# Experts' lists in another order, and expert 0's tokens in two halves, in a cross-attention and mixture-of-experts kernel

## The reference

```python
xn = xf / rms * norm_weight                      # 4096 x 256
logits = xn @ router_weight.T + router_bias      # 4096 x 16
probs = softmax(logits)
_, idx = jax.lax.top_k(logits.T, 256)            # per expert: 256 tokens
h = gelu(xn[idx] @ fc1_weight.T + fc1_bias)      # 256 x 1024 per expert
y = h @ fc2_weight.T + fc2_bias                  # 256 x 256
output = zeros.at[idx].add(y * gates); output /= sum of a token's gates
x = x + output
```

## Time and profile before

| | |
|---|---|
| median of three runs | 1154.19 us |
| profiled execution | 1155.01 us, its span 1153.2 us |
| PE busy | 1018.4 us, 88% of the span |
| DVE, ACT, POOL busy | 817.6, 669.7, 786.9 us |
| mean granted TensorE clock | 0.948 of full speed |

### The profile page before, as it was taken

One profiled execution on the slowest core, in us unless ns is written; L12 is line 12 of the kernel. 1 busy time (PEld: TensorE's weight loads), 2 busy tenths in 40 slices (PEclk: granted clock), 3 DMA queues, 4 the chain that ended last, 5 costly groups with the idle time before them and its releaser, 6 DMA issues.

```text
span 1153.2 us, 17657 instructions
## 1 busy us (share of the span) xinstructions
PE 1018.4 (88%) x6086; PEld 645.8 (56%) x6086; DVE 817.6 (71%) x1901; ACT 669.7 (58%) x1299; POOL 786.9 (68%) x880
## 2 busy tenths in 40 slices
PE   3779999999999999999998999998750499999996
PEld 2545445545645645554564555444320378999995
DVE  6886867976796786888769757785278756666642
ACT  6566675675586567748656765534424135666662
POOL 3117895896698679679678976977712168777773
PEclk9869999999999999999999999999965599999998
DMA  6020020010002002101200010010127146666652
GB/s 181 1 60 1 1 60 2 1 55 25 20 2 81 22 6 66 30 1 38 62 20 1 3 26 19 1 33 2 38 71 194 46 83 201 207 220 211 221 159 26
DMA packets 73817, 71.95 MB, mean 62 GB/s; under 512 B 38976, under 2 KB 67776, under 8 KB 69632
## 3 DMA queue, kind: packets, MB, share of 16 engines
q1 hardware_dynamic: 66608, 62.05, 17.1%
q0 software_dynamic: 6336, 8.70, 4.2%
q10 hardware_dynamic: 784, 0.07, 0.1%
HBM read 56.98 MB, written 13.83 MB: 61 GB/s over the span
## 4 chain that ended last, share of the span: by engine, by line
PE 73%; DVE 14%; POOL 4%; ACT 4%; issue 2%; DMA 1%; SPq 0%; ACTq 0%; DVEq 0%; POOLq 0%
PE bank L830 38%; PE score_pair L830 17%; PE pair_bank L830 12%; ACT probs L1128 3%; POOL prob_sum L1390 3%; PE bank L863 2%; DVE c_in L1800 2%; PE bank L911 2%; DVE root_t L1489 1%; DVE root_y L1491 1%; DVE maxima L1675 1%; DVE root_t L1490 1%; DVE in_stats L1496 1%; DMA c_in<-in_ctx 1%; DVE qk_nat L1649 1%
## 5 line engine op out<-in xcount | busy, mean ns | idle before, releaser
L1390 POOL TENSOR_TENSOR prob_sum<-prob_sum,probs 128x256 f32<-128x256 f32 x628 | 464.8, 771 | 77.4 <-ACT probs L1128 70.6
L1128 ACT ACTIVATE probs<-score_pair,mask_col 128x512 f32<-128x512 f32 x256 | 161.7, 683 | 117.5 <-PE score_pair L830 101.5
L1682 DVE CUSTOM_DVE_ANT_0 masked_scores<-pair_bank,mask_bias 128x512 bf16<-128x512 f32 x248 | 161.0, 686 | 85.3 <-PE pair_bank L830 84.8
L830 PE MATMUL bank<-probs,v_nat 128*64 128x512 f32 x768 | 206.3, 625 | 0.2 <-ACT probs L1128 0.2
L1675 DVE TENSOR_REDUCE maxima<-pair_bank 128x2 f32<-128x1024 f32 x62 | 75.8, 1223 | 45.9 <-PE pair_bank L830 45.8
L830 PE MATMUL score_pair<-q_hi,k_hi 64*128 64x512 f32 x384 | 91.3, 468 | 19.0 <-ACT probs L1128 17.6
L1128 ACT ACTIVATE probs<-score_pair 128x512 f32<-128x512 f32 x128 | 69.2, 592 | 65.5 <-PE score_pair L830 62.0
L830 PEld LDWEIGHTS score_pair<-q_hi,k_hi 64*128 64x128 f32 x384 | 37.2, 184 | 104.2 <-ACT probs L1128 55.7
L830 PE MATMUL pair_bank<-k_hi,q_hi 64*128 64x512 f32 x372 | 88.6, 471 | 5.4 <-DVE maxima L1675 2.4
L1368 POOL TENSOR_TENSOR z_lo<-z_full,z_hi 128x512 fp32r<-128x512 f32 x32 | 40.8, 1282 | 60.6 <-ACT z_hi L1128 60.6
L1461 POOL DMA_INDIRECT out_x<-y_out,token_index x32 | 55.1, 1722 | 39.1 <-DVE y_out L1985 34.2
(11 more groups left out here) (256 smaller groups left out, 2551.8 us busy)
## 6 DMA issues: line engine op xcount, KB each, us to landing
w_raw<-in_fc SPq DMA_DIRECT2D x16, 1024.0 KB, 4.8
w<-in_fc SPq DMA_DIRECT2D x16, 1024.0 KB
c_in<-in_ctx SPq DMA_DIRECT2D x16, 384.0 KB, 3.4
x_in<-in_x SPq DMA_DIRECT2D x8, 512.0 KB, 5.3
out_x<-x_in SPq DMA_DIRECT2D x8, 512.0 KB, 3.8
rows_scratch<-xr_nat SPq DMA_DIRECT2D x8, 512.0 KB, 3.0
c_in<-in_ctx SPq DMA_DIRECT2D x16, 128.0 KB, 3.4
b_rows<-in_fc_bias SPq DMA_DIRECT2D x16, 128.0 KB, 5.9
```

The source lines that it names most:

```text
L830: return pe.matmul(out, lhsT, rhs, start=start, stop=stop, skip_group_check=True)
L1128: return act.activation(out, a, f, bias=bias, scale=scale)
L1390: last = tt(total[:, half], first[:, half], p[:, half], ALU.add)
L1682: last = dve.tensor_tensor_reduce(masked[:, hh, :], place[:, hh, :], mask_bias[:, 512 * g:512 * (g + 1)], 1.0, MASKED, ALU.add, ALU.max, m ...
```

## The change

Parts 0 and 1 become experts 0 and 1 (64 columns), and the other fourteen (448 columns). Both first lists are made before anything of the others' slots. The chain up to the lists has fewer links: the limit's bits go straight into the tile that PE transposes, the marks read it from PSUM, the count of those above goes into the second rank as one more matmul (`rank(part, 1)`) instead of into two DVE operations. ACT makes one half of the ids for the first two groups (`ids_scaled`), and for group 0 both halves come in two pieces of 16 tiles. `list_join` is one operation, and the sum that it made moves behind the spread.

Expert 0's tokens are turned in halves, and its first four hidden pieces are done once for each half of 128 tokens (`hidden_part`). `order` is cut into `taken`, `order` and `rank`, which stand in other places. `turn_tokens(1)`, `scale_gates`, `renew_rows` and `split(2, 0)` stand ahead of expert 0's second product, `split(2, 1)` behind it. `EARLY` is 2.

```diff
-EARLY = 3
+EARLY = 2
...
-    def first_expert():
-
-        add("order", 1)
-        add("turn_tokens", 0)
-        add("slots", 1)
+    def first_lists():
+
+        add("limits")
+        add("taken", 0, 0)
+        add("order", 0, 0)
+        add("rank", 0, 0)
+        add("taken", 0, 1)
+        add("order", 0, 1)
+        add("rank", 0, 1)
+        add("keep_limits")
+        add("slots", 0)
+        add("list_hot", 0, 0)
+        add("list_hot", 0, 1)
+        add("list_count", 0)
+        add("list_join", 0)
+        add("list_spread", 0)
+        add("gather", 0)
         add("list_hot", 1, 0)
         add("list_hot", 1, 1)
-        for f in range(FT):
+        add("list_count", 1)
+        add("taken", 1, 0)
+        add("list_join", 1)
+
+    def first_expert():
+
+        add("turn_tokens", 0, 0)
+        add("order", 1, 0)
+        add("list_spread", 1)
+        add("gather", 1)
+        for f in range(2):
+            add("hidden_part", 0, f, 0)
+        add("turn_tokens", 0, 1)
+        for f in range(2, 4):
+            add("hidden_part", 0, f, 0)
+        add("rank", 1, 0)
+        for f in range(4):
+            add("hidden_part", 0, f, 1)
+        add("taken", 1, 1)
+        add("order", 1, 1)
+        add("rank", 1, 1)
+        add("slots", 1)
+        for f in range(4, FT):
             add("hidden", 0, f)
-            if f == 4:
-                add("list_count", 1)
-                add("list_join", 1)
-            elif f == 5:
-                add("list_spread", 1)
-                add("gather", 1)
-                add("scale_gates")
-                add("list_hot", 2, 0)
-                add("list_hot", 2, 1)
-                add("gather_gates", 0)
-                add("gather_gates", 1)
+        add("turn_tokens", 1)
+        add("scale_gates")
+        add("renew_rows")
+        add("split", 2, 0)
+        for part in range(2):
+            add("list_hot", 2, part)
+        for e in range(EARLY):
+            add("gather_gates", e)
         for c in range(2):
             for n, f in enumerate(OUT_ORDER[c]):
                 add("expert_out", 0, c, f)
...
                 elif c and n == 6:
                     add("list_spread", 2)
                     add("gather", 2)
-                    add("gather_gates", 2)
-                    add("renew_rows")
             add("gate", 0, c)
-            if c == 0:
-                add("turn_tokens", 1)
+        add("split", 2, 1)
 
     for r in range(SEARCH_ROUNDS):
         add("search", r)
         if r in FIRST_SPLITS:
             add("split", *divmod(FIRST_SPLITS.index(r), 2))
-    add("order", 0)
-    add("slots", 0)
-    for part in range(2):
-        add("list_hot", 0, part)
-    for piece in ("list_count", "list_join", "list_spread"):
-        add(piece, 0)
-    add("gather", 0)
+    first_lists()
...
             if at == (9 if e == 1 else 4):
                 for c in range(2):
                     add("scatter", e - 1, c)
-            if at == 1 and e == 1:
-                add("split", 2, 0)
-            if at == 9 and e + 1 < E:
+            if at == 9 and 2 < e + 1 < E:
                 add("split", e + 1, 1)
             if at == 13 and e + 2 < E:
...
+        def limits():
+            on.wait_ge(attention_done, 4)
+            on.wait_ge(choice_consts, 1)
+            on.wait_ge(*order_ready.at("wide"))
+            pe.transpose(bank[1][:, 0:E], wide[:], ident[0:E, 0:E]).then_inc(searched.sem, 1)
+
+        def rank(part, n):
+
+
             experts = experts_of[part]
             columns = slice(experts.start * NT, experts.stop * NT)
-            if part == 0:
-                on.wait_ge(attention_done, 4)
-                on.wait_ge(choice_consts, 1)
-                on.wait_ge(*order_ready.at("wide"))
-                pe.transpose(bank[1][:, 0:E], wide[:], ident[0:E, 0:E]).then_inc(searched.sem, 1)
-            else:
+            flat = lambda t: t[:].rearrange("p e j -> p (e j)")[:, columns]
+            if part:
                 on.wait_ge(*slots_made.at(0))
-            flat = lambda t: t[:].rearrange("p e j -> p (e j)")[:, columns]
-            for n, taken in enumerate((above, equal)):
-                on.wait_ge(*order_ready.at("tiles", part, n))
-                mm(order_bank[n][:, columns], before[:], flat(taken), True, False)
-                mm(order_bank[n][:, columns], all_ones[:], earlier[:, columns], False, True).then_inc(searched.sem, 1)
-                if n == 0:
-                    totals = running[:].rearrange("p (e j) -> p e j", j=NT)[:, experts, NT - 1]
-                    mm(list_bank[:, total_place][:, experts], all_ones[:], totals, True, True).then_inc(searched.sem, 1)
+            on.wait_ge(*order_ready.at("tiles", part, n))
+            if n:
+                totals = running[0][:, experts, NT - 1:NT].broadcast_to([P, experts.stop - experts.start, NT])
+                mm(order_bank[n][:, columns].rearrange("p (e j) -> p e j", j=NT), all_ones[:], totals, True, False)
+            mm(order_bank[n][:, columns], before[:], flat(kinds[n]), n == 0, False)
+            mm(order_bank[n][:, columns], all_ones[:], flat(earlier[n]), False, True).then_inc(searched.sem, 1)
...
+        def list_hot(g, part):
+
+            if part and g < 2:
+                on.wait_ge(*rests_marked.at(g))
+                for at in list_tiles(g):
+                    func(hot_ids[:, at, 0:1, 0, :], hot_lo[:, at, 0:1, :], ACT.Identity,
+                         scale=token_in_tile[:, 0:1]).then_inc(ids_scaled.sem, 1)
+
...
+        def up(e, f, c=None):
+
             i = e % 2
-            on.wait_ge(*xe_emptied.at(e))
+            on.wait_ge(*xe_emptied.at(*token_key(e, c)))
             for n in range(2):
                 on.wait_ge(*w_lo_made.at(e, n))
-            n = e * FT + f
+            n = hidden_turn[e, f]
             if n >= 4:
                 on.wait_ge(*h_made.at(*hidden_order[n - 4]))
-            to, cols, n = hidden_bank[n % 4][:, 0:CAP], slice(f * P, (f + 1) * P), 0
+            tokens = slice(0, CAP) if c is None else slice(c * P, (c + 1) * P)
+            to, cols, n = hidden_bank[n % 4][:, tokens], slice(f * P, (f + 1) * P), 0
             for half in range(2):
                 for w, x in ((w1_hi, xe_hi), (w1_lo, xe_hi), (w1_hi, xe_lo)):
-                    last = mm(to, w[i][:, half, cols], x[i][:, half, :], n == 0, n == 5)
+                    last = mm(to, w[i][:, half, cols], x[i][:, half, tokens], n == 0, n == 5)
                     n += 1
-            last.then_inc(hidden_filled.sem, 1)
+            return last
+
+        def hidden(e, f):
+            up(e, f).then_inc(hidden_filled.sem, 1)
+
+        def hidden_part(e, f, c):
+            last = up(e, f, c)
+            if c:
+                last.then_inc(hidden_filled.sem, 1)
...
+
+        def limits():
+
+            on.wait_ge(attention_done, 4)
+            on.wait_ge(choice_loaded, 16 * N_CHOICE)
+            ts(wide[:].bitcast(U32), low_bits[0:E, :].broadcast_to([E, P]), high_bits[0:E, :], limit_flip[0:E, :],
+               ALU.bitwise_or, ALU.bitwise_xor).then_inc(order_ready.sem, 1)
+
+        def keep_limits():
+
+            on.wait_ge(*searched.at("limits"))
+            dve.tensor_copy(limit[:], bank[1][:, 0:E]).then_inc(limits_kept, 1)
...
-            parts = list_parts[0:16 * n, 0:n]
             on.wait_ge(*listed.at(g))
-            settle(tt(parts.rearrange("p i a x -> p (i a x)"), list_bank[0:16 * n, 0:32 * n],
-                      own_block[0:16 * n, 0:n, :].rearrange("p i x -> p (i x)"), ALU.mult))
-            stt(list16[0:16 * n, 0:n, :], parts[:, :, 1, :], float(P), parts[:, :, 0, :], ALU.mult,
-                ALU.add).then_inc(joined.sem, 1)
+            tt(list_parts[0:16 * n, 0:n].rearrange("p i a x -> p (i a x)"), list_bank[0:16 * n, 0:32 * n],
+               own_block[0:16 * n, 0:n, :].rearrange("p i x -> p (i x)"), ALU.mult).then_inc(joined.sem, 1)
 
```

More of the change, by code:

```diff
@@ L770, in _build @@
             if at[1]:
-                ids_made.will(at[0])
+                for part in range(len(list_tiles(at[0]))):
+                    ids_made.will(at[0], part)
+                    if at[0] < 2:
+                        ids_scaled.will(at[0], part)
+            else:
+                rests_marked.will(at[0])
         elif kind == "list_count":
@@ L783, in _build @@
             xe_emptied.will(*at)
[L784 to L788, removed]
+        elif kind == "hidden" or kind == "hidden_part" and at[2]:
+            hidden_filled.will(*at[:2])
+            hidden_order.append(tuple(at[:2]))
+            h_made.will(*at[:2])
+            if in_parts(*at[:2]):
                 h_hi_made.will(*at)
@@ L818, in _build @@
     searched.will("limits")
-    for part in range(2):
-        for piece in (("order", part, 0), ("totals", part), ("order", part, 1)):
-            searched.will(*piece)
-    experts_of = (slice(0, 1), slice(1, E))
-    order_bank, total_place = bank[5:7], slice(P, P + E)
+    for kind, *at in expert_plan:
```

(28 more changed lines are left out.)

146 lines of the change are left out of this document (80 added, 66 removed).

## The result

The changed kernel takes 1160.97 us (median of 19 executions, 1156.57 to 1164.46), the one before, beside it, 1155.52 (19, 1153.41 to 1157.71): ratio 1.0047, 95% interval [1.0035, 1.0059]. The prediction, 1152.3 with a range to 1157.4, was wrong: the forecast did not come, and the rival in which the clock comes late came, larger than I had priced it. The profiled execution took 1160.71 us, its span is 1158.9.

The account below looks back on a forecast made before the run. PE, busy throughout from 968.9 us, bounds, so expert 2's start decides: 4.4 us gained, 2.6 left after halves, a 4.4 us stall; expert 2 0.4 earlier, expert 3 1.85 earlier; 1153.15 profiled, 1152.3 us median, range 1148.3 to 1157.4.

Parts of the forecast that it names:

- the rival in which the clock comes late: Expert 0's hidden pieces: half passes do little to raise the clock; 4.2 us more, 1156.5, at upper bounds 1158.3; chance 0.27.
- Index and first pass: Chain to the first list and gather: index 1.0 us earlier; PE needs only the first gather, first pass 4.4 us earlier.
- Price of a half pass: Expert 0's passes of 128 tokens: 0.115 us each at full clock, 0.213 at half clock; 24 passes more.
- The rival that prices halves by columns: PE takes half passes at 0.107 and 0.06 us; time 1149.8, or 1148.5 without the SBUF collision; chance 0.22.
- Less 0.4 because the clock should rise about 5 us after the first pass: Expert 0's hidden pieces: clock rises short of the 24th half pass, 0.4 us off; sum 11.8, end at 923.1.
- The collision with the gates: POOL's subtraction from `split(2, 0)` holds a two-input DVE operation in the gates: 1.3 us more (bounds 0 and 2.4).
- The stall at the count: PE, ready at 929.5, waits for list 2's ids; count begins at 933.95; a stall of 4.4 us.
- I charge 1.8: Clock lost in the stall before expert 1: 1.8 us (bounds 0 and 2.3), first pass of expert 1 at 938.5.
- Expert 1 in 14.1 us, expert 2 not waiting: Expert 1 takes 14.1 us (bounds 13.4 and 15.4); POOL is ready, so expert 2 starts at 952.6.
- the 16 that the prediction named as a sign of being wrong: Expert 1's duration: the prediction called itself wrong if it took under 13 us or over 16.

Follow-up runs that it names:

- half5: all_four with expert 5's 8 hidden pieces in 96 half passes of 128 columns instead of 48 whole ones; 1153.69 us, ratio 0.9986.
- wide_halves: Changed kernel with the same 48 passes in the place of expert 0's half passes, each with 256 columns; 1156.18 us, ratio 1.0001.
- split20_later: Changed kernel with the split of expert 2's first half of weights moved behind the gathers of the gates; 1157.79 us, ratio 1.0015.
- turn1_later: Changed kernel with expert 1's tokens turned behind expert 0's first 16 second products, as in the kernel before; 1155.31 us, ratio 1.0005.
- fill_short: Changed kernel with 9 unused products (18 passes) on PE in its wait for list 2's ids; 1154.98 us, ratio 0.9998.
- whole0: Changed kernel with expert 0's first four hidden pieces in whole passes of 256 tokens, both turns still halves; 1156.02 us, ratio 0.9993.
- all_four: Changed kernel with expert 0 in whole passes, expert 1's tokens turned later, and expert 2's and 3's first-half weight splits moved later; 1148.49 us, ratio 0.9942.
- three_wide: all_four with expert 0 in half passes again, but each 256 columns wide; 1148.78 us, ratio 0.9943.
- three_halves: all_four with expert 0 in half passes again; 1152.59 us, ratio 0.9979.

## Why the prediction was wrong, step by step

- **Index and first pass: right.** The index was 0.9 us earlier (forecast 1.0; 8.3 instead of 9.1 behind the common zero), the first pass 4.3 us earlier (forecast 4.4). That PE needs only the first gather held.
- **Price of a half pass: right.** 0.21 us at half clock, 0.112 at full (I took 0.115). The Trainium skill's figure in TensorE: Matmul & The Clock Gate, Back-to-back issue gap, 81 ns, did not hold for this form; half5 shows 112. The rival that prices halves by columns is refuted.
- **"Less 0.4 because the clock should rise about 5 us after the first pass": this is the step that failed.** It rose 14.2 us after it, behind the last half pass, although PE had no gap in all that time. I had read 4.0 us of whole passes in the kernel before and carried them to half passes; wide_halves shows that the columns made the difference. The hidden pieces ended at 928.0 instead of 923.1 (4.4 us net of the shifted zero); the rival's price was 4.2.
- **The collision with the gates: right in kind,** 1.0 us for 1.3 (split20_later).
- **The stall at the count: right,** 4.2 us for 4.4. I had put down its cause as the gates' length and POOL; a part is DVE's place for expert 1's tokens, as turn1_later brings the gates 2.9 us forward.
- **"I charge 1.8" for the clock in the stall (bounds 0 and 2.3): far too little.** By fill_short it is 6.0 us. Directly it is 2.3 from the count to expert 1 (5.1 instead of 2.8) and 1.3 in expert 1; most of the rest comes through a term that the sum had at nothing.
- **Expert 1 in 14.1 us, expert 2 not waiting: wrong by 2.4.** It took 16.5, past the 16 that the prediction named as a sign of being wrong. I had checked that POOL's weights come in time (they did: 949.6 us) and not what the next split, expert 3's, stands beside. It met DVE's ids of list 3 in 955.33 to 959.4, and the tokens of expert 2 behind them.

The sum again, from the table: the count came 4.1 us later than forecast (late clock 4.4, the smaller collision less 0.3), expert 1 0.5 more (5.1 instead of 2.8 and the charged 1.8), expert 2 another 2.4 (16.5 instead of 14.1: slow passes 1.3, wait 1.7, less 0.6 that expert 1 otherwise stayed under my 14.1). That is 7.0, and expert 3 began 7.0 later. With the zero's own 0.5 us it makes 7.5 of the 7.6 between 1153.15 and the profiled 1160.71.

The rival had the first of these terms and stopped at 1158.3, as it too had expert 1 end with its own work.

## What to carry to other kernels

Cutting a pass in two for an earlier start is paid twice where the weight load sets the pace: in loads, and in a clock that may not rise; price the halves at the clock of the place where they run, and ask whether the work behind them is what raises it. A wait that begins in a stretch at full clock can cost more than its length (here filling it gave 6.0 us for a wait of 4.2): look what runs in the 10 us behind it, and try filler work or another order of the other engine's queue before shortening anything. And where one edit shifts an engine by some us, check every later place where a two-input DVE operation runs beside a POOL subtraction, not only the one that the edit moved.

## What was not expected of the hardware

- 48 half passes (128 columns, PE busy without a gap) ran at 1.2 GHz for 11 us without raising the clock, while 96 of them, begun at 2.4 GHz, did not lower it in 10.7 us (half5). The same kind of pass kept the higher clock there and did not raise the lower one here.
- The clock fell within a wait of 4.2 us, some 2 us after it began, and stayed down for 10 us, 8 us of them behind its end; in whole0's profiled execution a wait of the same length cost 3.4 us of slow clock. In the profiled executions the clock fell at every wait of 2.0 to 4.2 us for the count, and in all_four, three_wide, three_halves and half5, where PE waited 0.6 to 1.2 us, it stayed.
- One kernel's executions lie up to 8 to 12 us apart (whole0 1148.2 to 1159.7, turn1_later 1153.2 to 1161.4). How long the clock stays down may be a part of it, but that isn't shown: wide_halves has the wait and spreads over 4.9 us, three_halves has 0.6 us of it and spreads over 5.3, and two executions of whole0 with almost the same mean clock took 1150.4 (0.950) and 1157.0 (0.951).
- A DVE product of two bf16 inputs (1.22 us alone) took 4.08 us beside POOL's subtraction of 2.37, more than both one after the other (3.59).
